# Keys and queries of the first stage as three float32r products of split weights and rows, with the next chunk's rows turned between key and query product

## What is computed

```python
h = _layernorm(x, axis=-1) * (1 + ca) + sa
q = (x @ Wq + bq).reshape(b, s, H, HD).transpose(0, 2, 1, 3)   # x is h here
k = (x @ Wk + bk).reshape(b, s, H, HD).transpose(0, 2, 1, 3)
v = (x @ Wv + bv).reshape(b, s, H, HD).transpose(0, 2, 1, 3)
mask = cols <= rows + WINDOW
scores = jnp.einsum('bhqd,bhkd->bhqk', q, k) / jnp.sqrt(jnp.float32(HD))
```

## Time and profile before

| what | value |
|---|---|
| median of 3 runs | 2086.68 us (2086.62 to 2087.52) |
| the profiled execution's own time | 2084.18 us |
| its span in the trace | 2082.4 us |
| first stage: first normalisation of the chunk loop to the next stage's first load | 34.5 us to 151.3 us of the span |
| mean granted TensorE clock over the span | 0.939 of full speed |
| busy over the whole span: PE, ACT, DVE | 88%, 64%, 22% |

### The profile page before, as it was taken

How to read it: one execution, slowest core, us unless ns; L and a number is a source line. 1 busy time by engine, 2 the same in 40 slices (tenths; PEclk the granted TensorE clock), 3 DMA queues, 4 the chain that set the end, 5 groups by cost and what they waited for, 6 DMA issues and landing times. The chain is left out here.

```text
span 2082.4 us, 47224 instructions
## 1 busy us (share of the span) xinstructions
PE 1842.0 (88%) x18361; PEld 937.0 (45%) x18362; DVE 456.9 (22%) x1360; ACT 1327.4 (64%) x1633; POOL 290.1 (14%) x329
## 2 busy tenths in 40 slices
PE   4863899999999999999999999665499999999995
PEld 3542333333333333333333333554266676767674
DVE  4655000000000000000000000345233333333331
ACT  2432789998999989999899999222133333333331
POOL 1000110001100011100010000365121212121211
PEclk9995899999999999999999999666699999999998
DMA  4336320000400004000000000863412121221223
GB/s 136 121 130 138 58 60 10 10 10 17 80 17 10 9 18 80 18 10 10 10 25 10 17 2 2 313 222 124 137 33 33 33 33 33 33 34 32 34 32 97
DMA packets 83823, 116.06 MB, mean 56 GB/s; under 512 B 9372, under 2 KB 75612, under 8 KB 83036
## 3 DMA queue, kind: packets, MB, share of 16 engines
q1 hardware_dynamic: 66616, 90.97, 15.4%
q0 software_dynamic: 13296, 17.80, 5.0%
q10 hardware_dynamic: 3760, 5.03, 0.9%
HBM read 73.03 MB, written 40.74 MB: 55 GB/s over the span
## 5 line engine op out<-in xcount | busy, mean ns | idle before, releaser
L1063 ACT ACTIVATE at_probs<-at_scores 128x1536 f32<-128x1536 f32 (+2 forms) x756 | 1023.0, 1436 | 57.9 <-PE at_scores L965 52.7
L965 PE MATMUL at_scores<-at_q_rows,kept_k_rows 99*32 99x512 bf16 (+3 forms) x9920 | 618.6, 363 | 34.6 <-ACT at_probs L1063 17.0
L982 PE MATMUL at_out<-at_probs,kept_v 128*17 128x512 f32 (+3 forms) x4832 | 587.6, 566 | 5.0 <-DVE at_out_T L1076 5.0
L965 PEld LDWEIGHTS at_scores<-at_q_rows,kept_k_rows 99*32 99x32 bf16 x9920 | 238.4, 96 | 560.7 <-ACT at_probs L1063 343.3
L1770 ACT ACTIVATE ex_hT<-ex_ps_hT,kept_b 128x128 f32<-128x128 f32 x568 | 154.2, 383 | 375.9 <-PE ex_ps_hT L1727 375.9
L1716 PE MATMUL ex_ps_h<-kept_w,ex_xT 128*128 x568 | 260.1, 601 | 0.9 <-DVE ex_xT L1785 0.9
L1735 PE MATMUL ex_ps_y<-kept_w,ex_hT 128*128 x1136 | 258.7, 381 | 2.5 <-ACT ex_hT L1770 2.5
L1076 DVE COPY at_out_T<-at_out 128x512 f32<-128x512 f32 x32 | 22.1, 691 | 972.0 <-PE at_out L982 972.0
L1735 PEld LDWEIGHTS ex_ps_y<-kept_w,ex_hT 128*128 128x128 f32 x1136 | 211.5, 191 | 28.9 <-issue 2.7
L1048 POOL TENSOR_SCALAR_AFFINE_SELECT at_probs<-at_probs 128x512 f32<-128x512 f32 (+2 forms) x156 | 83.1, 541 | 1010.0 <-ACT at_probs L1063 1008.4
L982 PEld LDWEIGHTS at_out<-at_probs,kept_v 128*17 128x17 f32 x4832 | 127.2, 98 | 131.1 <-DVE at_out_T L1076 20.3
(11 more groups left out here) (206 smaller groups left out, 928.2 us busy)
## 6 DMA issues: line engine op xcount, KB each, us to landing
kept_w<-in_W SPq DMA_DIRECT2D x16, 1024.0 KB, 9.8
ex_x_tile<-queue SPq DMA_DIRECT2D x72, 129.5 KB, 2.0
k_parts<-kparts SPq DMA_DIRECT2D x8, 768.0 KB, 3.7
q_parts<-qparts SPq DMA_DIRECT2D x8, 768.0 KB, 3.7
at_q_rows<-q_parts SPq DMA_DIRECT2D x32, 192.0 KB
kept_k_rows<-k_parts SPq DMA_DIRECT2D x4, 1120.0 KB
x_rows<-in_x SPq DMA_DIRECT2D x4, 1024.0 KB, 14.0
kept_k_rows<-k_parts SPq DMA_DIRECT2D x8, 512.0 KB
```

The costliest lines, as they stand in the source:

```text
L965: ins = nc.tensor.matmul(ps_s[b:b + CT, c % 2, at:at + part], k_rows[:, k + b:k + b + CT], q_rows[:, q:q + part], start=True, stop=True)
L982: ins = nc.tensor.matmul(ps_o[h * CT:h * CT + HD + 1, first:C], v[:, kb, g * GH + h, :], probs[:, slot, column:column + width], start=i == ...
L1063: nc.scalar.activation(probs[:, c % RING, 0:width], ps_s[:, c % 2, 0:width], ACT.Exp).then_inc(exped, 1)
```

## The change

Key and query weights are split once, by POOL in the prologue, into a float32r copy and the float32r remainder (`wk_high`, `wk_low`, `wq_high`, `wq_low`). A chunk's rows are split in the same way: ACT writes `hT_high` (float32r) and then `hT` (float32) from `ps_turn`, and DVE subtracts the two into `hT_low`, which has one buffer. Keys and queries are then high·high + high rows with low weights + low rows with high weights, each with float32r operands; the product of the two low parts is left out. The values are made as before from `hT`.

On PE the turn of the next chunk stands between a chunk's keys and its queries. ACT normalises two chunks ahead, applies the modulation one chunk ahead, and takes the queries out last. The loops over chunks of SP, ACT, PE and DVE are written out, without hardware loops. The store of the ones rows is made in eight pieces instead of one, from a smaller buffer. Cut to its core:

```diff
+        hT_high = sb("hT_high", [P, 2, KD, C], F32R)
+        hT_low = sb("hT_low", [P, 1, KD, C], F32R)
+        wk_high, wk_low, wq_high, wq_low = (sb(n, [P, KD, D], F32R) for n in ("wk_high", "wk_low", "wq_high", "wq_low"))
-        ones_rows = sb("ones_rows", [3 * H, S], BF16)
+        ones_rows = sb("ones_rows", [3 * H, C], BF16)
...
+            for w, high in ((wk_turned, wk_high), (wq_turned, wq_high)):
+                nc.gpsimd.tensor_copy(high[:], w[:]).then_inc(pool_step, 1)
+            pool.wait_ge(pool_step, 8 + 2 * KD)
+            for w, high, low in ((wk_turned, wk_high, wk_low), (wq_turned, wq_high, wq_low)):
+                nc.gpsimd.tensor_tensor(low[:], w[:], high[:], ALU.subtract).then_inc(pool_step, 1)
...
+            def modulate(c):
+                u = c % 2
+                if c >= 2:
+                    act.wait_ge(v_ready, c - 1)
+                act.wait_ge(turned, c + 1)
+                for k in range(KD):
+                    nc.scalar.activation(hT_high[:, u, k, :], ps_turn[:, k, :], ACT.Identity,
+                                         scale=mod_cols[:, 2 + k:3 + k],
+                                         bias=mod_cols[:, k:k + 1]).then_inc(high_ready, 1)
+                for k in range(KD):
+                    nc.scalar.activation(hT[:, u, k, :], ps_turn[:, k, :], ACT.Identity,
+                                         scale=mod_cols[:, 2 + k:3 + k],
+                                         bias=mod_cols[:, k:k + 1]).then_inc(h_ready, 1)
...
+            normalise(0)
+            normalise(1)
+            modulate(0)
+            for c in range(NC):
+                keep_one(c, 0, kf, ps_k, 1.0, bk)
+                if c + 1 < NC:
+                    modulate(c + 1)
+                if c + 2 < NC:
+                    normalise(c + 2)
+                keep_one(c, 1, qf, ps_q, HD ** -0.5, bq_scaled)
...
+            def project(c, n_out, w_high, w_low, ps):
+                u = c % 2
+                pe.wait_ge(high_ready, (c + 1) * KD)
+                if c > 0:
+                    pe.wait_ge(kq_kept, (2 * (c - 1) + n_out + 1) * KD)
+                for m in range(KD):
+                    cols = slice(m * P, (m + 1) * P)
+                    for n, (w, x_part) in enumerate(((w_high, hT_high), (w_low, hT_high), (w_high, hT_low))):
+                        if n == 2:
+                            pe.wait_ge(low_ready, c + 1)
+                        for k in range(KD):
+                            last = nc.tensor.matmul(ps[:, m, :], w[:, k, cols], x_part[:, 0 if n == 2 else u, k, :],
+                                                    start=n == 0 and k == 0, stop=n == 2 and k == KD - 1)
+                last.then_inc(k_ready, 1)
...
+            turn(0)
+            for c in range(NC):
+                project(c, 0, wk_high, wk_low, ps_k)
+                if c + 1 < NC:
+                    turn(c + 1)
+                project(c, 1, wq_high, wq_low, ps_q)
+                values(c)
...
+            def split_low(c):
+                u = c % 2
+                dve.wait_ge(h_ready, (c + 1) * KD)
+                if c > 0:
+                    dve.wait_ge(k_ready, 2 * c)
+                nc.vector.tensor_tensor(hT_low[:, 0], hT[:, u], hT_high[:, u], ALU.subtract).then_inc(low_ready, 1)
...
+            split_low(0)
+            for c in range(NC):
+                split(c, 0, kf, kparts, k_stored)
+                if c + 1 < NC:
+                    split_low(c + 1)
+                split(c, 1, qf, qparts, q_stored)
+                dve.wait_ge(v_ready, c + 1)
+                nc.vector.tensor_tensor(v[:, c * CB:(c + 1) * CB, :, 0:HD],
```

More of the change, by code:

```diff
@@ L9 @@
 F32 = mybir.dt.float32
+F32R = mybir.dt.float32r
 BF16 = mybir.dt.bfloat16
@@ L246, in _ @@
             act.wait_ge(act_step, 3)
[L248 to L277, removed]
@@ new lines, in keep_one @@
+            def keep_one(c, n, full, ps, scale, bias):
+                act.wait_ge(k_ready, 2 * c + n + 1)
+                if c > 0:
+                    act.wait_ge(parts_ready, 2 * c - 1 + n)
+                for m in range(KD):
+                    nc.scalar.activation(full[:, m, :], ps[:, m, :], ACT.Identity, scale=scale,
+                                         bias=bias[:, m:m + 1]).then_inc(kq_kept, 1)
+            normalise(0)
[8 more added lines that the diff above has]
+                keep_one(c, 1, qf, ps_q, HD ** -0.5, bq_scaled)
@@ L295, in _ @@
             pe.wait_ge(act_step, 3)
[L296 removed]
+            pe.wait_ge(pool_step, 10 + 2 * KD)
             pe.wait_ge(w_in, 16 * 6)
[L298 to L305, removed]
[L306 to L325 removed]
@@ new lines, in values @@
+            def values(c):
+                u = c % 2
+                pe.wait_ge(h_ready, (c + 1) * KD)
+                if c > 0:
+                    pe.wait_ge(v_kept, c)
+                for j in range(CB):
+                    for k in range(KD):
+                        last = nc.tensor.matmul(ps_v[:, j, :], hT[:, u, k, j * P:(j + 1) * P], wv[:, k, :],
+                                                start=k == 0, stop=k == KD - 1)
+                last.then_inc(v_ready, 1)
+            turn(0)
@@ L413, in _, with split @@
-            dve.wait_ge(v_kept, NC + 1)
+            def split(c, n, full, parts, kept):
+                u = c % 2
+                dve.wait_ge(kq_kept, (2 * c + n + 1) * KD)
+                if c >= 2:
+                    dve.wait_ge(kept[u], 16 * (c // 2))
+                step.inc(nc.vector.tensor_copy(parts[:, u, 0], full[:]))
+                step.wait(dve)
+                step.inc(nc.vector.tensor_tensor(full[:], full[:], parts[:, u, 0], ALU.subtract))
+                step.wait(dve)
+                step.inc(nc.vector.tensor_copy(parts[:, u, 1], full[:]))
+                step.wait(dve)
+                nc.vector.tensor_tensor(parts[:, u, 2], full[:], parts[:, u, 1],
+                                        ALU.subtract).then_inc(parts_ready, 1)
@@ L415, in over_tiles @@
+            dve.wait_ge(v_kept, NC)
 def over_tiles(eng, body):
```

93 lines of the change are left out of this document (41 added, 52 removed).

## The result

The changed kernel takes **2069.06 us**, median of 6 runs (2066.16 to 2074.83), the kernel before 2087.65 us (6 runs, 2086.62 to 2089.61). The ratio is 0.9914, 95% interval [0.9898, 0.9929]: faster, by 18.6 us. The profiled execution took 2067.55 us, with a span of 2065.8 and a mean granted clock of 0.932.

What follows compares the result with a forecast made beforehand. PE was taken as the longest engine, 13.22 us a chunk with 1.61 of waiting. Seven new periods of 10.1 plus 1.2 make 71.9 us instead of 92.44, so 2086.68 - 20.5 = 2066.2 us, range 2062 to 2075.

Steps and rivals of the forecast that it cites:

- One f32r matmul, 0.222 us: Keys and queries on PE: one record per float32r matmul, 24 a chunk, 5.33 us instead of 6.96.
- Rivals 1 to 4: Time per float32r matmul: 0.41 us, chance 0.04; 0.43, chance 0.05; 0.26 to 0.32, chance 0.10; 0.34 to 0.37, chance 0.03.
- The turn's place removes 1.61 us: Turn between keys and queries: ACT's passes run beside queries and values, so PE's 1.61 us wait for `hT` goes.
- DVE becomes the bound at 10.1 us: First-stage chunk on DVE: splits 3.86 + 3.85, values 1.22, low rows 1.2; longest engine, just ahead of PE's 9.97.
- First to eighth split 71.9 us: First stage, first to eighth key split: 7 x 10.1 + 1.2 = 71.9 us instead of 92.44.
- The start is unchanged, with 0.9 either way: Before the first key split: first keys end at 44.8 to 46.4 us against 45.5; no change taken.
- Waits for the low rows are covered: PE's wait for `hT_low` within the keys: the loop through the subtraction takes 8.5 us, below 10.1.
- The next stage near 131: End of the first stage: the next stage's first load comes near 131 us, before at 151.33.
- That tail, and every later stage, waits for the block to end, so it moves with the eighth split.: Behind the first stage: the last split's store and all later stages move along with the 20.5 us saved.
- Written-out loops cost nothing I can see: First-stage code without the hardware loop: no cost or gain, up to 2 us left on the slow side.

Runs made afterwards that it cites:

- the turn alone: New order of the turn with plain float32 products and no split of rows or weights, timed against the kernel before: 2077.31 us, ratio 0.9957.
- the other one: Profiled execution of the changed kernel timed once more, unchanged, on another occasion: 2067.96 us, ratio 0.9907, attention 1079.2 us.
- the pad: Changed kernel plus 64 one-column matmuls on PE behind the first stage's last value product: 2067.99 us, one run, attention 1080.93.
- the spread load: Changed kernel with the next head group's four key DMAs issued behind tiles 3 to 6, not all behind tile 3: 2058.16 us; once more 2059.47.
- the two spread kernels: Key-load DMAs issued over four tiles in the changed kernel, 2058.16 us, and in the kernel before, 2082.73 us.

## Why the prediction was right, and where it was not

- **One f32r matmul, 0.222 us.** Right: 0.23. The price came from the value rows, the nearest in weights and streaming. Rivals 1 to 4 fall with it. Weight loads of 0.188 to 0.206 us run beside records 0.23 us apart, so the Trainium skill's rule (TensorE: Matmul & The Clock Gate, Part 3, on what overlaps), by which a load runs beside a matmul only in another row group, is not what these rows show: full 128-row loads are hidden.
- **The turn's place removes 1.61 us.** Right, and the turn alone gave 2.0 of the 3.25 us a chunk, since PE's items also follow each other more closely (11.19 a chunk against 11.61 busy).
- **DVE becomes the bound at 10.1 us.** Right, at 9.97: key split 3.85, low rows 1.13, query split 3.85, values 1.14, each from start to start. The prediction took 1.2 and 1.22 for the low rows and the values, durations that include their ends. PE's own need is 9.8 (keys 2.92 as between 52.82 and 55.74, queries 2.83, turn 0.79, values 3.27), so relief of DVE alone could give 0.2 a chunk.
- **First to eighth split 71.9 us.** 70.58: 10.77 + 6 x 9.97 and rounding.
- **The start is unchanged, with 0.9 either way.** Right: 0.5 later. The first keys ended at 45.94, within the 44.8 to 46.4 given.
- **Waits for the low rows are covered.** Nearly: the pair of records with the low rows takes 0.57 us to the next instead of 0.46, about 0.1 a chunk.
- **The next stage near 131.** 129.98.
- **"That tail, and every later stage, waits for the block to end, so it moves with the eighth split."** This is the step that failed. The stages behind don't only move: the attention gave back 5.45 us in the profiled execution (2.6 in the other one). In the first stage the forecast was 0.85 us too careful (20.5 for 21.35); the median came out 2.9 us above it (2069.06 for 2066.2), so errors of both signs partly cancel, and that the total came so near is in part luck. Beside it stands "Written-out loops cost nothing I can see": I looked at what a loop costs where it runs, while the length of the code matters where it shifts the fetches of what follows. The 5.45 us are made, near enough, of 2.8 more of issue gaps, 1.2 more of waiting for query rows (10.8 for 9.6), and 1.6 more of PE's busy time (1040.16 for 1038.57 over the stretch), which goes with the clock. The gaps are shown to be the change's doing, by the pad, the spread load and the places above; the other two terms differ between executions of one kernel. In the medians the give-back is 21.35 - 18.6 = 2.7 us.

Open are four things. The waits for query rows also differ between the two spread kernels (11.2 and 9.1), so they differ without the fetches. With the pad, one gap kept its place, which the theory doesn't explain, and why a gap is 1.4 us long in one run and 4.4 in another is not shown. The stretch behind the attention took 784.7 to 789.3 us in these profiles, with no pattern that a change explains. And the 24.6 us between the two spread kernels are 2.5 more than their stage ends account for, which is within what single medians scatter.

## What to carry to other kernels

Price a new kind of operation from the row nearest to it in shape, add up each engine's chunk, and read the new period from the longest sum; here that came within 0.13 us. Before taking the later stages as merely moved, look for places where they wait for no one: here a bulk load that fills the DMA engines also held up instruction fetches, and a change of code length far ahead moved PE into that hole. Splitting the load into pieces with pauses between them cost a few lines and gave 8.5 us after the change and some 4 in the kernel before.

## What was not expected of the hardware

- While 3 MB of keys came in, no instruction packet arrived for 16 us (one every 7 to 9 us in the 52 us ahead and behind); PE ran dry for 1.4 to 4.4 us, and behind some of these gaps its clock fell to the 1.2 GHz level (0.54 over 7.4 us in the change), behind others not.
- With two waits of 1.4 to 1.6 us a chunk, records went from 0.23 to 0.42 us in some chunks (granted clock 0.89 over such a chunk) and not in others (1.00).
- A DVE cast of 0.69 us takes 2.7 to 2.9 beside a POOL subtraction of 2.4 to 3.2 us: here the work handed to POOL was taken from DVE.
- The first products after 14.65 us of standing still run at half pace whether the view shows the granted clock as 0.50, as after the change, or as 1.00, as in the padded run (records 0.42 us apart in both).
